# Linear attention inside an eight-layer kernel: squares summed a pair later, value rows between the key transposes, two chains of inverse norms, output projection summed pair by pair

## The reference, cut to what matters

```python
keys    = l2norm((x @ Wk) per head)          # row / max(norm, 1e-12)
values  = (x @ Wv) per head
queries = l2norm((x @ Wq) per head)
beta    = sigmoid(x @ Wbeta)
log_retain = log(1 - beta + 1e-8);  cum_log = cumsum(log_retain)
decay   = exp(min(cum_log[t] - cum_log[s], 0)) * (s >= t)
weights = (queries @ keys.T) / sqrt(64) * decay
out     = weights @ values + beta * values
y       = out.reshape(t, 16 * 64) @ Wout
```

## Time and profile before

| | |
|---|---|
| median of 3 runs | 4981.29 us (4979.67 to 5001.24) |
| the profiled execution | 4969.21 us, of which the trace spans 4967.5 us |
| busy, share of the span | PE 90%, PEld 56%, DVE 48%, ACT 35%, POOL 17% |
| mean granted TensorE clock | 0.912 of full speed |
| one turn | about 615 us, of which the linear attention some 100 us |

### The profile page before, as it was taken

How to read it: one execution, slowest core, us unless ns; L and a number is a source line. 1 busy time by engine, 2 the same in 40 slices (tenths; PEclk the granted TensorE clock), 3 DMA queues, 4 the chain that set the end, 5 groups by cost and what they waited for, 6 DMA issues and landing times.

```text
span 4967.5 us, 76834 instructions
## 1 busy us (share of the span) xinstructions
PE 4473.0 (90%) x30219; PEld 2776.4 (56%) x30275; DVE 2379.6 (48%) x6906; ACT 1719.1 (35%) x3496; POOL 843.7 (17%) x1441
## 2 busy tenths in 40 slices
PE   7998989889898898988989889899898998989989
PEld 3556645565455654556545575455754457545575
DVE  3435634356443554435544355444554445544455
ACT  2322432325333343333433234333343333433334
POOL 2003110031100311103011040111401114011130
PEclk8989979999899998999989999899998999998989
DMA  2000000000000000000000000000000000000000
GB/s 68 1 1 1 1 6 1 1 1 1 6 1 1 1 1 6 1 1 1 1 6 1 1 1 1 6 1 1 2 1 6 1 1 2 1 3 1 1 1 3
DMA packets 19571, 17.25 MB, mean 3 GB/s; under 512 B 2462, under 2 KB 18799, under 8 KB 19183
## 3 DMA queue, kind: packets, MB, share of 16 engines
q1 hardware_dynamic: 19183, 11.99, 0.8%
HBM read 9.89 MB, written 2.10 MB: 2 GB/s over the span
## 4 chain that ended last, share of the span: by engine, by line
PE 80%; DVE 6%; POOL 6%; ACT 5%; issue 3%; DVEq 0%; ACTq 0%; POOLq 0%; SPq 0%
PE banks L984 7%; PE banks L974 7%; PE banks L988 7%; PE banks L880 7%; PE banks L908 6%; PE banks L825 6%; PE banks L920 3%; POOL work L478 3%; PE banks L865 3%; PE banks L1180 3%; PE banks L1201 2%; PE banks L1167 2%; PE banks L1074 2%; PE banks L1047 2%; PE banks L1023 2%
## 5 line engine op out<-in xcount | busy, mean ns | idle before, releaser
L1369 DVE CUSTOM_DVE_ANT_0 work<-banks,mask_row 128x512 f32<-128x512 f32 (+3 forms) x1024 | 451.6, 488 | 274.0 <-PE banks L880 270.6
L880 PE MATMUL banks<-work 32*128 32x512 f32 (+3 forms) x2048 | 526.7, 493 | 11.4 <-DVE work L1369 11.4
L908 PE MATMUL banks<-work 32*128 32x256 f32 (+3 forms) x2048 | 512.7, 504 | 20.8 <-ACT work L638 20.8
L638 ACT ACTIVATE work<-banks 128x384 f32<-128x384 f32 (+1 forms) x768 | 368.9, 526 | 441.9 <-PE banks L908 440.3
L437 POOL TENSOR_TENSOR rstd<-rstd,half 128x2 f32<-128x2 f32 x128 | 87.5, 703 | 2451.2 <-DVE moments L1297 1834.2
L654 ACT ACTIVATE work<-banks 128x512 f32<-128x512 f32 (+1 forms) x384 | 228.8, 596 | 687.6 <-PE banks L984 687.4
L1441 DVE TENSOR_TENSOR work<-work,banks 128x512 f32<-128x512 f32 (+1 forms) x384 | 263.5, 686 | 344.8 <-PE banks L988 344.5
L984 PE MATMUL banks<-xnT,wg 128*128 128x512 f32 (+1 forms) x768 | 417.8, 627 | 0.0
L988 PE MATMUL banks<-xnT,wu 128*128 128x512 f32 (+1 forms) x768 | 406.1, 611 | 0.0
L447 POOL TENSOR_SCALAR_AFFINE_SELECT work<-work 128x128 f32<-128x128 f32 (+1 forms) x768 | 252.6, 332 | 897.4 <-ACT work L638 886.1
L974 PEld LDWEIGHTS banks<-wd,work 128*128 128x128 f32 (+1 forms) x3072 | 360.6, 191 | 57.3 <-issue 57.3
(11 more groups left out here) (255 smaller groups left out, 7254.4 us busy)
## 6 DMA issues: line engine op xcount, KB each, us to landing
x_next<-in_L_attn_a_x_dram SPq DMA_DIRECT2D x8, 256.0 KB, 2.8
out_dram<-x SPq DMA_DIRECT2D x8, 256.0 KB, 2.2
wg<-in_L_ffn_Wg_dram SPq DMA_DIRECT2D x1, 1376.0 KB
wu<-in_L_ffn_Wu_dram SPq DMA_DIRECT2D x1, 1376.0 KB
wd<-in_L_ffn_Wd_dram SPq DMA_DIRECT2D x2, 512.0 KB
wk_l<-in_L_attn_a_Wk_dram SPq DMA_DIRECT2D x1, 512.0 KB, 7.8
wv_l<-in_L_attn_a_Wv_dram SPq DMA_DIRECT2D x1, 512.0 KB, 6.5
wq_l<-in_L_attn_a_Wq_dram SPq DMA_DIRECT2D x1, 512.0 KB, 7.2
```

The lines of the kernel that those rows point to most:

```text
L638: eng.activation(prob4[:, G % 2, hh, C_AT[j]:C_AT[j] + C_N[j]], bank(3 + c % 3)[:, 0:C_N[j]], ACT.Exp).then_inc(s_exp, 1)
L880: m = eng.matmul(bank(k % 3)[:, col:col + N], q4[own, G, P * t:P * t + P], k4[own, G, 0:N], start=True, stop=True)
L908: m = eng.matmul(bank(3 + c % 3)[:, col:col + N], k4[own, G, P * s:P * s + P], q4[own, G, P * s:T], start=True, stop=True)
L1369: m = eng.tensor_tensor_reduce(out=summed[:, k % 2, col:col + N], in0=bank(k % 3)[:, col:col + N], in1=mask_row[:, T - N:T], scale=1.0, sc ...
```

## The change

TensorE: the sums of squares of pair j are issued after the products and key transposes of pair j + 1, the last of them between the key transposes 4 and 5. Value rows 0 and 1 go between the last key transposes, in banks 6 and 7 instead of 2 and 3, so that they no longer wait for all copies of the keys. The output projection becomes `project_out(c)`, one pair's share of all four tiles: pairs 0 to 4 after `transposes(5)`, pair 5 after `transposes(6)`, pairs 6 and 7 at the end; the matmuls are the same 32.

ScalarE: two square roots of 64 values per row, the queries' after value row 2, the keys' after value row 5, in place of one of 128.

VectorE: the copy of the queries' sums moves forward to between the key copies. The chain of inverse norms becomes two of 64 values: the keys' ahead of `scale_values(0)`, the queries' inside the loop, after `scale_values(2)` and ahead of `sum_states(0)`.

```diff
@@ act_lin @@
-            for i in range(2):
+            for i in range(3):
                 value_rows(i)
             eng.wait_ge(l_ssc, 1)
-            eng.activation(l_inv[:, :, :, :], l_ssum[:, :, :, :], ACT.Sqrt).then_inc(l_norm, 1)
-
-            for i in range(2, NC2):
+            eng.activation(l_inv[:, 0, :, :], l_ssum[:, 0, :, :], ACT.Sqrt).then_inc(l_norm, 1)
+            for i in range(3, 6):
+                value_rows(i)
+            eng.wait_ge(l_ssk, NC2)
+            eng.activation(l_inv[:, 1, :, :], l_ssum[:, 1, :, :], ACT.Sqrt).then_inc(l_norm, 1)
+            for i in range(6, NC2):
                 value_rows(i)
@@ pe_lin @@
-                if i % 2 == 1:
-                    sum_squares(i // 2)
-            for i in range(NT, 2 * NT):
-                key_rows(i)
-            eng.wait_ge(l_kr, NC2)
-            for i in range(NC2):
+                if i >= 3 and i % 2 == 1:
+                    sum_squares(i // 2 - 1)
+
+            def value_rows(i):
                 if i >= 2:
                     eng.wait_ge(l_vr, i - 1)
-                eng.matmul(bank(2 + i % 2), xnT[:, P * (i % NT):P * (i % NT) + P],
+                else:
+                    eng.wait_ge(l_be, 1)
+                eng.matmul(bank(6 + i % 2), xnT[:, P * (i % NT):P * (i % NT) + P],
                            wv_l[:, 512 * (i // NT):512 * (i // NT) + 512],
                            start=True, stop=True).then_inc(l_vp, 1)
+
+            key_rows(NT)
+            sum_squares(NC2 - 1)
+            key_rows(NT + 1)
+            value_rows(0)
+            key_rows(NT + 2)
+            value_rows(1)
+            key_rows(NT + 3)
+            for i in range(2, NC2):
+                value_rows(i)
@@ states @@
-                    eng.wait_ge(l_vr, NC2)
+                    eng.wait_ge(l_kr, NC2)
@@ pe_lin @@
+            def project_out(c):
+
+                eng.wait_ge(l_oTs, c + 1)
+                for t in range(NT):
+                    m = eng.matmul(bank(t // 2)[:, P * (t % 2):P * (t % 2) + P], l_kT[:, c, P * t:P * t + P],
+                                   wout_l[:, c, :], start=(c == 0 and t % 2 == 0), stop=(c == NC2 - 1),
+                                   skip_group_check=True)
+                    if c == NC2 - 1 and t % 2 == 1:
+                        m.then_inc(l_y, 1)
...
-            eng.wait_ge(l_oTs, NC2)
-            for t in range(NT):
-                for c in range(NC2):
-                    m = eng.matmul(bank(t // 2)[:, P * (t % 2):P * (t % 2) + P], l_kT[:, c, P * t:P * t + P],
-                                   wout_l[:, c, :], start=(c == 0), stop=(c == NC2 - 1))
-                if t % 2 == 1:
-                    m.then_inc(l_y, 1)
+                if c == NC2:
+                    for i in range(NC2 - 3):
+                        project_out(i)
+                if c == NC2 + 1:
+                    project_out(NC2 - 3)
+            project_out(NC2 - 2)
+            project_out(NC2 - 1)
@@ lin @@
+                    if i == NT + 1:
+                        eng.wait_ge(l_ss, NC2)
+                        eng.tensor_copy(l_ssum[:, 0, :, :].rearrange("p t h -> p (t h)"),
+                                        bank(5)[:, 0:NT * H]).then_inc(l_ssc, 1)
...
+                def inverse_norms(w, done):
+                    eng.wait_ge(l_norm, done)
+                    inv, rec, ssum = l_inv[:, w, :, :], l_rec[:, w, :, :], l_ssum[:, w, :, :]
+                    link(eng.tensor_scalar(inv, inv, 1e-18, None, ALU.max))
+                    link(eng.reciprocal(rec, inv))
+                    link(eng.tensor_tensor(rec, rec, ssum, ALU.mult))
+                    link(eng.tensor_tensor(inv, inv, rec, ALU.add))
+                    link(eng.tensor_scalar(inv, inv, 0.5, None, ALU.mult))
+
+                    link(eng.tensor_scalar(inv, inv, 1e-12, None, ALU.max))
+                    link(eng.reciprocal(inv, inv))
+
+                inverse_norms(1, 2)
...
                     mask_scores(c)
                     if c + 2 < NC2:
                         scale_values(c + 2)
+                    if c == 0:
+                        inverse_norms(0, 1)
+                        link(eng.tensor_scalar(l_inv[:, 0, :, :], l_inv[:, 0, :, :], float(DM) ** -0.5, None,
+                                               ALU.mult))
                     sum_states(c)
```

More of the change, by code:

```diff
@@ L663, in value_rows @@
                 half, t = i // NT, i % NT
-                eng.activation(l_v[:, t, 512 * half:512 * half + 512], bank(2 + i % 2), ACT.Copy).then_inc(l_vr, 1)
+                eng.activation(l_v[:, t, 512 * half:512 * half + 512], bank(6 + i % 2), ACT.Copy).then_inc(l_vr, 1)
             for i in range(2 * NC2):
@@ L1464, in lin @@
                 reduce_keys(NC2 - 1)
[L1465 to L1470, removed]
-                link(eng.tensor_scalar(l_inv[:, :, :, :], l_inv[:, :, :, :], 1e-18, None, ALU.max))
-                link(eng.reciprocal(l_rec[:, :, :, :], l_inv[:, :, :, :]))
-                link(eng.tensor_tensor(l_rec[:, :, :, :], l_rec[:, :, :, :], l_ssum[:, :, :, :], ALU.mult))
-                link(eng.tensor_tensor(l_inv[:, :, :, :], l_inv[:, :, :, :], l_rec[:, :, :, :], ALU.add))
-                link(eng.tensor_scalar(l_inv[:, :, :, :], l_inv[:, :, :, :], 0.5, None, ALU.mult))
-                link(eng.tensor_scalar(l_inv[:, :, :, :], l_inv[:, :, :, :], 1e-12, None, ALU.max))
-                link(eng.reciprocal(l_inv[:, :, :, :], l_inv[:, :, :, :]))
-                link(eng.tensor_scalar(l_inv[:, 0, :, :], l_inv[:, 0, :, :], float(DM) ** -0.5, None, ALU.mult))
+                def inverse_norms(w, done):
[9 more added lines that the diff above has]
+                inverse_norms(1, 2)
                 def scale_values(c):
```

## The result

The changed kernel takes 5063.31 us, the median of four runs from 5024.67 to 5090.13; the kernel before took 4980.48 beside them (4968.94 to 5001.24). The ratio is 1.0156, with a 95% interval of 1.0081 to 1.023. All ratios in this document leave out runs that lie more than 1.5% above the fastest of their kernel, so they need not be the quotients of the medians. The forecast was 5227: the direction was right, the size three times too large (246 us for 83).

The account below looks back on a forecast made before the run. TensorE, 80% of the last chain, was taken as the bound. Gains of 2.6 us a turn against 33.4 lost to half clock left 30.8, times eight 246, giving 5227 us against the median; range 4990 to 5265.

Parts of the forecast that it names:

- Sums of squares: Making of queries and keys: TensorE's waits for ScalarE's squares go, a gain of 2.6 us a turn.
- Value rows, both chains, the pause: From `key_rows(4)` to `outputs(0)`: start at 20.05 us after a 2.65 us TensorE pause, 0.6 us a turn lost.
- The bounded cost of VectorE beside GpSimd: Second chain, beside GpSimd's product: extra VectorE time between 0 and 0.85 us; taken 0.5 for the scaling, 0.3 for a link.
- Projection: From `outputs(7)` on: pair by pair gains 1.2 us, a later addition loses 0.6, net gain 0.6 us a turn.
- the loop over pairs runs at half clock to its end, in all turns: Linear attention from `outputs(0)` to `outputs(7)`: the clock falls in the pause and stays down, costing 33.4 us a turn; chance 0.66.
- the 1.7 us within which the clock was to fall: Start of the loop: the clock may fall up to 1.7 us after `outputs(0)` starts, so 33.4 us instead of 34.26.
- falls but soon rises: Rival for the loop: the clock falls but recovers soon, 4972 to 4982 us, up to 5000; chance 0.10.
- half clock in a part of the turns or of the loop: Rival for the loop: half clock only in some turns or part of it, 4993 to 5194 us; chance 0.14.

Follow-up runs that it names:

- e4: The kernel before with only the sums of squares a pair later and the projection pair by pair; 4970 us, ratio 0.9982.
- e1: The changed kernel with the queries' chain of inverse norms moved from ahead of the first sum of states to behind the second; 4888 us, ratio 0.9826.
- e5: The changed kernel with the pause ahead of `outputs(0)` filled by two useless value rows on TensorE; 4912 us, ratio 0.9876.
- e6: The kernel before with only the new value rows, two square roots and two chains of inverse norms; 5141 us, ratio 1.0333.
- e3: The changed kernel with ten small linked VectorE instructions, about 2.6 us, ahead of each turn's first norm; 5105 us, ratio 1.024.
- e2: The kernel before with ten small linked VectorE instructions, about 2.6 us, ahead of each turn's first norm; 5016 us, ratio 1.0114.
- e9: e6 with four useless value rows right behind `outputs(1)`; 5093 us, ratio 1.0249.
- e10: e6 with the matmuls of `outputs(1)` done three times, twice into a bank nobody reads; 5173 us, two runs of 5134 and 5212.
- e7: e1 with ten small linked VectorE instructions, 2.6 us, ahead of each turn's first norm; 4973 us, ratio 0.9998.

## Why the prediction was right in direction and wrong in size

*Sums of squares.* Right, and somewhat better than forecast: no idle time is left before them. A pair takes 2.61 us in the first half (1642.97 less 1640.36) where it took 3.36 (1604.43 less 1601.07, the sums of pairs 2 and 3 before), and 3.05 for 3.37 in the second: 3 times 0.75 and 4 times 0.32 are 3.5 us a turn where I had 2.6. I had counted the idle time alone, and the 0.29 us of the second half stood in a row of the weight load (PEld), not of the matmuls, which have no idle time there; a sum after a wait also took 1.05 us for 0.95, and what followed it started later. In e4 the last sum, now among the key transposes, covers about 0.8 us of the wait for VectorE's copies as well; with the projection's 0.9 this makes the 5.1 to 5.7 us.

*Value rows, both chains, the pause.* Right in each step: `outputs(0)` 19.68 us after `key_rows(4)` (forecast 20.05), a pause of 2.68 us (2.65), value rows waiting 0.93 (0.9), one table load for both roots. That load took 1.28 us with the root 0.01 us behind it in every kernel here; the price of the Trainium skill (ScalarE: Activation LUTs, What ACT_TABLE_LOAD costs) of about 2.66 us does not show. The bounded cost of VectorE beside GpSimd was 0.69 on the scaling (1.34 less 0.65; taken 0.5) and 0.25 on one link (taken 0.3, on another link).

*Projection.* From `outputs(7)` to the next norm's first transposes (L793) it takes 17.25 us where it took 18.19 (before, L790 at 1691.67): net 0.94, forecast 0.6.

*The step that failed* is the forecast's own: "the loop over pairs runs at half clock to its end, in all turns", 33.4 us a turn. The fall was right: the clock falls behind the pause, in all eight turns; with the pause cut to 0.56 us (e1) or filled (e5) it does not fall. How long it stays down was not: in the profiled execution it stayed at half to the loop's end in no turn, in turn 1 the loop cost 22.3 us more (58.53 less 36.19), and in seven turns 4.83. The price was too high as well: where the clock did stay down to the end (e6, turn 3) the loop cost 28.8 us more. No row of before shows the 1.7 us within which the clock was to fall; in turn 3 it fell in the row that begins 0.74 us behind the start of `outputs(0)`. By the rival "falls but soon rises" the time would have come to 4972 to 5000, so that rival came near in the layer, in seven turns, and was wrong in the time. I gave one outcome for all turns 0.66 and the other 0.10, as if the kernel decided between them; a part of the turns or of the loop, which is what came, had 0.14. e3 shows that the kernel does not decide it: in turns 2, 3 and 6 of one execution, with the same loop and the same pause, the stretch at half lasted 48 us, to the loop's end, and 10 us.

*What had no term at all* is the larger part: 104 of the profiled 121 us lie in the two attention layers. The prediction's own rows showed it: the same stretch of the third layer at 14.18 us in turn 1 and 9.17 in turn 3. I used these rows to say that a busy TensorE stays at half clock, and did not ask what they say of the sum: that a turn's other layers are not constant, and that a change which moves their start can cost or give 7 to 10 us for each, eight times over. e2 shows this without any change to the layer. So the direction was right by luck for the most part: the layer that the forecast was about is 17.2 us longer over all eight turns, and the rest comes from layers that it had left out.

The range held the time, since the rival "half clock in a part of the turns or of the loop" reached down to 4993; that is luck too, as its price came from the wrong layer.

The rule of the Trainium skill (TensorE: Matmul & The Clock Gate, Part 1, What's actually happening), that the default is throttled and activity releases it, was named as standing for the rival that rises. The runs agree with it in e9, where the clock rose during four value rows, and not in e6, where it stayed at 0.50 through 61.60 us of matmuls in 63.53 us. The same section says that the point of the change varies with where a kernel's first matmul lands in a window that the chip watches; here too the point varies, from turn to turn (e3), but no run shows what sets it.

**Open.** Why the clock came back after 10 us in most turns of the changed kernel, after 38 in e10 and not at all in most of e6 is not settled beyond what e3 shows: the length goes with the point of `outputs(0)` at which the clock fell. What sets that point, and why a slightly earlier fall (0.92 us for 0.80 in the same row) keeps the clock down to the end, no run shows. Nor is it shown why the attention layers were at 88 us in nearly all turns of the changed kernel and not at 78 or 81; that their start decides it is shown only so far as a delay alone (e2, e7) changes them. Nor is it shown why the four runs of the changed kernel spread over 65 us; only one was profiled.

## What to carry to other kernels

A pause of 2.7 us ahead of a long loop of small matmuls can cost ten times its length (28.8 us in a turn of e6): look for what VectorE has queued ahead of the instruction that the loop waits for, and move it behind (e1), or fill it with matmuls that nobody reads (e5, two value rows). Before a gain of a few us a turn is believed, sum the layers that were not touched, in all turns: here they moved by up to 10 us each and hid a gain of 46 us in e4. Measure a change in such a kernel with a small shift as well (e2, e3, e7), since a lucky or unlucky start can be larger than the change.

## What the runs showed of the hardware that was not expected

The same pause can be harmless or not, in the same layer. Timeline of the kernel before, third layer of turn 3, PE:

```profile
1454.14 2.79 PE L880 MATMUL banks<-work 32*128 32x256 f32 x10 [0.71 <-DVE work L1369]
1456.86 0.66 PE L892 MATMUL banks<-ident,work 128*128 128x128 f32 x4
```

and of the changed kernel, the same layer and turn:

```profile
1486.25 2.86 PE L883 MATMUL banks<-work 32*128 32x256 f32 x10 [0.71 <-DVE work L1392]
1489.04 1.12 PE L895 MATMUL banks<-ident,work 128*128 128x128 f32 x4
```

Both wait 0.71 us and then do the same ten matmuls; in one kernel the four transposes behind them take 0.66 us, in the other 1.12, and the clock is at half for the next 13 us. And a turn's pattern can lock: turns 2 to 7 of the changed kernel lasted 631.3 to 631.6 us each, with the fall of the clock in `outputs(0)` at the same place to 0.02 us, while e4's turns alternated between 610 and 625 us. A delay of 2.58 us did not always lengthen a turn: turns 5 to 7 of e2 took 614.4 us, as turns 3 to 5 of the kernel before did, since the first attention layer was 2.5 us shorter.
